# Attention loop's first iterations: bias vector by row sums, coupling ahead of the loop, value/output product over three iterations

## The reference, cut to what matters

```python
q = query @ Wq.T + bq                  # query = layernorm(x)
k = mem_state @ Wk.T + bk
v = mem_state @ Wv.T + bv
scores = einsum('btd,bsd->bts', q, k) / sqrt(d)   # only the 32 largest stay
attn = softmax(scores)
x = x + (attn @ v) @ Wo.T + bo
...
kernels = exp(-alpha * t) * cos(omega * t + phi)
kernels = kernels / clip(sum(abs(kernels)), 1e-8)
coupling = softmax(field_coupling)     # 16 x 16, mixes the heads of the wave
...
scale = max(mean(abs(W)), 1e-8)        # of each ternary weight
```

## Time and profile before

| what | value |
|---|---|
| three runs | 475.23, 476.73, 477.58 us (median 476.73) |
| the profiled execution | 476.81 us, of which its span is 474.9 |
| mean granted clock of TensorE | 0.996 |
| busy: PE, DVE, ACT, POOL | 450.1, 324.3, 253.7, 226.3 us |
| busy of PE's weight loads | 353.5 us |
| chain that ended last | PE 62%, DVE 20%, ACT 6%, issue 5%, POOL 4%, DMA 3% |

### The profile page before, as it was taken

One profiled execution on the slowest core, in us unless ns is written; L12 is line 12 of the kernel. 1 busy time (PEld: TensorE's weight loads), 2 busy tenths in 40 slices (PEclk: granted clock), 3 DMA queues, 4 the chain that ended last, 5 costly groups with the idle time before them and its releaser, 6 DMA issues.

```text
span 474.9 us, 6229 instructions
## 1 busy us (share of the span) xinstructions
PE 450.1 (95%) x2146; PEld 353.5 (74%) x2146; DVE 324.3 (68%) x582; ACT 253.7 (53%) x391; POOL 226.3 (48%) x265
## 2 busy tenths in 40 slices
PE   6999898899999899897899999999989999999996
PEld 2578565678888787685688888888768888888884
DVE  4899679698999899864898893655763322433223
ACT  1887857678888786673787546442551111211111
POOL 5703198379779767951000681334326653333330
PEclk9999999999999999899999999999999999999999
DMA  7997813153334324364372300000000000010002
GB/s 231 413 366 253 311 46 132 46 177 105 125 126 142 125 90 128 137 222 177 146 218 81 112 1 22 1 0 0 1 1 0 1 0 1 24 65 1 0 1 88
DMA packets 22814, 48.93 MB, mean 103 GB/s; under 512 B 2176, under 2 KB 2176, under 8 KB 21760
## 3 DMA queue, kind: packets, MB, share of 16 engines
q1 hardware_dynamic: 22784, 48.55, 29.1%
HBM read 46.44 MB, written 2.10 MB: 102 GB/s over the span
## 4 chain that ended last, share of the span: by engine, by line
PE 62%; DVE 20%; ACT 6%; issue 5%; POOL 4%; DMA 3%; DVEq 0%; SPq 0%; ACTq 0%; POOLq 0%
PE bank L1179 9%; PE bank L1181 9%; PE bank L1180 9%; PE bank L1584 6%; PE bank L1598 6%; PE bank L1600 6%; PE bank L1585 6%; DVE mt_lo L945 3%; PE bank L1194 3%; DMA ctxr<-ctx 3%; DVE work L958 2%; POOL nat_lo L418 2%; DVE mx L954 2%; PE bank L1186 2%; PE bank L1272 2%
## 5 line engine op out<-in xcount | busy, mean ns | idle before, releaser
L418 POOL TENSOR_TENSOR nat_lo<-ctxr,nat_hi 128x512 fp32r<-128x512 f32 x64 | 83.4, 1330 | 21.3 <-ACT nat_hi L600 20.9
L757 ACT ACTIVATE g<-bank,b1c 128x512 f32<-128x512 f32 x32 | 22.1, 691 | 91.2 <-PE bank L1600 91.2
L1159 DVE CAST g_hi<-g 128x512 fp32r<-128x512 f32 x32 | 13.7, 427 | 76.9 <-ACT g L757 76.8
L471 POOL TENSOR_SCALAR w2s<-w2t 128x512 fp32r<-128x512 int8 x32 | 19.9, 622 | 68.2 <-PE bank L1585 68.2
L1584 PE MATMUL bank<-w2s,g_lo 128*128 128x512 f32 x128 | 50.2, 392 | 1.8 <-DVE g_lo L1161 1.8
L1598 PE MATMUL bank<-xt_lo,w1s 128*128 128x512 f32 x128 | 50.8, 397 | 0.0
L1600 PE MATMUL bank<-xt_hi,w1s 128*128 128x512 f32 x128 | 50.7, 396 | 0.0
L1585 PE MATMUL bank<-w2s,g_hi 128*128 128x512 f32 x128 | 50.2, 392 | 0.0
L576 ACT ACTIVATE mt_hi<-bank 128x512 fp32r<-128x512 f32 x64 | 37.8, 596 | 20.2 <-PE bank L1350 19.7
L945 DVE TENSOR_TENSOR mt_lo<-bank,mt_hi 128x512 fp32r<-128x512 f32 x64 | 43.6, 682 | 5.9 <-ACT mt_hi L576 5.5
L1350 PEld LDWEIGHTS bank<-ident,ctxr 128*128 128x128 f32 x256 | 30.5, 141 | 15.4 <-DMA ctxr<-ctx 4.9
(11 more groups left out here) (233 smaller groups left out, 1204.0 us busy)
## 6 DMA issues: line engine op xcount, KB each, us to landing
ctxr<-ctx SPq DMA_DIRECT2D x32, 512.0 KB, 3.5
wab<-w1T SPq DMA_DIRECT2D x4, 1024.0 KB, 10.9
wab<-w2T SPq DMA_DIRECT2D x4, 1024.0 KB, 5.5
wgraw<-wgT SPq DMA_DIRECT2D x4, 1024.0 KB, 5.4
wst<-w1T SPq DMA_DIRECT2D x4, 1024.0 KB, 4.8
wst<-w2T SPq DMA_DIRECT2D x4, 1024.0 KB, 5.4
resid<-x SPq DMA_DIRECT2D x4, 512.0 KB, 6.5
out<-resid SPq DMA_DIRECT2D x8, 256.0 KB, 2.2
```

What stands on the lines that cost most here:

```text
L418: pool.tensor_tensor(nat_lo[:, par, c, :], ctxr[:, b % 4, c, :], f(nat_hi[:, par, c, :]), ALU.subtract).then_inc(nat_lo_ok, 1)
```

## The change

The bias vector's product is formed by row sums: DVE scales and adds the rows of `woraw` into `sum_k` (`xbias_sum`, four operations, ahead of the loop), and PE sums that over the partitions with one matmul against ones, now into bank 3 and after `score(0)`. The vector goes to a free tile `xn[:, 1]`, and POOL adds it to one tile of `resid` at the end of each iteration 1 to 8. The coupling's matmul goes ahead of `q_product(6)`, `mix_part` ahead of `kern`. In iteration 0 `norms` goes before `chunk(3)`. Of `wvo`, four matmuls go to iteration 0 (after `score` of steps 5 to 7), eight to iteration 1, four stay in iteration 2; quarter 1 goes to bank 4 and the quarters 0, 2 and 3 to bank 5, so quarter 3 waits for `wvo_lo_ok` 3. The sums of the ternary scales go to the head of iteration 1, and `turn_prob(0)` to its end.

```diff
+        def wvo_bank(d):
+            return bank[4 if d == 1 else 5]
...
POOL
-            def attn_bias(ts):
-                for t in ts:
+            def attn_bias(t):
+                if 0 <= t < NT:
                     pool.wait_ge(xbias_ok, 1)
                     pool.wait_ge(ln_ready, t + 1)
-                    pool.tensor_tensor(resid[:, t, :], resid[:, t, :], bias_x[:, :], ALU.add).then_inc(xres_ok, 1)
+                    pool.tensor_tensor(resid[:, t, :], resid[:, t, :], xn[:, 1, :], ALU.add).then_inc(xres_ok, 1)
...
                 split_q(i + 1, 0)
-                if i == 0:
-                    attn_bias(range(NT))
                 nat_lo_part(i - 1, 1)
+                attn_bias(i - 1)
...
ACT
                 mt_hi_part(0)
-                if i == 2:
-                    wvo_hi_part(2)
+                if i in (1, 2):
+                    wvo_hi_part(2 * i - 2)
...
                 nat_hi_part(i - 1, 1, (0, 1))
-                mt_hi_part(6)
                 if i == 1:
                     wvo_hi_part(1)
+                mt_hi_part(6)
...
DVE
+            def xbias_sum():
+                dve.wait_ge(wo_in, 16)
+                dve.wait_ge(qbias_ok, 1)
+                for o in range(DC):
+                    row_sum(sum_k, woraw, 2, o).then_inc(sums_ok, 1)
+                    dve.wait_ge(sums_ok, DC + o + 1)
...
             for t in range(4):
                 token_part(t)
+            mix_part()
... (kern, habs and its absolute value as before)
+            xbias_sum()
...
iteration 0 of DVE, before: m0 t4 m1 t5 m2 xbias m3 t6 t7 m4 mix m5 m6 norm ctok m7 sum_rows
iteration 0 of DVE, after:  m0 t4 m1 t5 m2 t6 m3 t7 ctok m4 xbias m5 norm m6 m7 sum_rows
(m = mt_lo_part, t = token_part; in iteration 1 wvo_lo_part(0) follows scales, wvo_lo_part(1) goes before m6)
-                    if p == 0:
-                        dve.wait_ge(xres_ok, NT)
+                    dve.wait_ge(xres_ok, p + 1)
...
PE
             for n in range(3, 2 * DC):
+                if n == 6:
+                    pe.wait_ge(cpr_ok, 2)
+                    pe.wait_ge(qbias_ok, 1)
+                    pe.matmul(bank[4][:, 0:H], cpr[0:H, :], ident[0:H, 0:H], start=True, stop=True).then_inc(coup_ps, 1)
                 q_product(n)
             def x_bias():
-                for o in range(DC):
-                    ins = pe.matmul(bank[4][:, :], cols[:, 2, o:o + 1].to_broadcast([P, P]), woraw[:, o, :], ...)
+                pe.wait_ge(sums_ok, 2 * DC)
+                pe.wait_ge(q_ok, 2 * DC)
+                pe.matmul(bank[3][:, :], ones[:, :].to_broadcast([P, P]), sum_k[:, :], start=True,
+                          stop=True).then_inc(xbias_ps, 1)
...
             def wvo_step(d, vs):
+                if d == 0 and vs[0] == 0:
+                    pe.wait_ge(wo_in, 16)
+                    pe.wait_ge(wv_in, 16)
+                    pe.wait_ge(ctok_sum, NT)
+                if d == 1 and vs[0] == 0:
+                    pe.wait_ge(mix_ok, 1)
+                    pe.wait_ge(norm_ok, 1)
+                    pe.wait_ge(scale_ok, 1)
+                if d >= 2 and vs[0] == 0:
+                    pe.wait_ge(wvo_lo_ok, 1 if d == 2 else 3)
...
             def wvo_in_turn(i, j):
+                if i == 0 and j >= 5:
+                    wvo_step(0, ((0,), (1,), (2, 3))[j - 5])
                 if i == 1:
                     if j == 0:
+                        totals()
+                    elif j < 4:
+                        wvo_step(1, ((0,), (1, 2), (3,))[j - 1])
                     else:
+                        wvo_step(2, (j - 4,))
                 if i == 2 and j < 2:
                     wvo_step(3, (2 * j, 2 * j + 1))
...
-                if i == 2:
-                    turn_prob(0)
...
                 join(i - 2, 1)
-                if i != 1:
-                    turn_prob(i - 1)
+                turn_prob(i - 1)
```

More of the change, by code:

```diff
@@ L512, in wvo_hi_part @@
                 act.wait_ge(wvo_ps, d + 1)
-                act.activation(wvo_hi[:, d, :], bank[4 + d % 2][:, :], ACT.Copy).then_inc(wvo_hi_ok, 1)
+                act.activation(wvo_hi[:, d, :], wvo_bank(d)[:, :], ACT.Copy).then_inc(wvo_hi_ok, 1)
             def first_tiles(ts):
@@ L895, in xbias_part @@
                 dve.wait_ge(bo_in, 16)
-                dve.tensor_tensor(bias_x[:, :], bias_x[:, :], bank[4][:, :], ALU.add).then_inc(xbias_ok, 1)
+                dve.wait_ge(ctok_sum, NT)
+                dve.tensor_tensor(xn[:, 1, :], bias_x[:, :], bank[3][:, :], ALU.add).then_inc(xbias_ok, 1)
             def mix_part():
@@ L915, in wvo_lo_part @@
                 dve.wait_ge(wvo_hi_ok, d + 1)
-                dve.tensor_tensor(wvo_lo[:, d, :], bank[4 + d % 2][:, :], f(wvo_hi[:, d, :]),
+                dve.tensor_tensor(wvo_lo[:, d, :], wvo_bank(d)[:, :], f(wvo_hi[:, d, :]),
                                   ALU.subtract).then_inc(wvo_lo_ok, 1)
@@ L997, in _ @@
                 if i == 0:
-                    token_part(6)
                     token_part(7)
-                if i == 1:
-                    wvo_lo_part(0)
+                    dve.wait_ge(ctok_sum, NT)
+                    dve.tensor_scalar(ctok[:, :], ctok[:, :], qbias[:, DC:DC + 1], None, ALU.add).then_inc(ctok_ok, 1)
+                    dve.wait_ge(ctok_ok, 1)
                 if i == 2:
@@ L1006, in _ @@
                 if i == 0:
-                    mix_part()
+                    xbias_part()
                 top8(i - 1, 2)
                 mt_lo_part(5)
-                top8(i - 1, 3)
-                mt_lo_part(6)
                 if i == 0:
                     norm_part()
-                    dve.wait_ge(ctok_sum, NT)
-                    dve.tensor_scalar(ctok[:, :], ctok[:, :], qbias[:, DC:DC + 1], None, ALU.add).then_inc(ctok_ok, 1)
-                    dve.wait_ge(ctok_ok, 1)
+                top8(i - 1, 3)
+                if i == 1:
+                    wvo_lo_part(1)
+                mt_lo_part(6)
                 p = i - 1
@@ L1265, in norms, with totals @@
                 pe.wait_ge(mix_ok, 1)
-                pe.matmul(bank[4][:, 0:P], ones[:, :].to_broadcast([P, P]), habs[:, :, :].rearrange("p h c -> p (h c)"),
-                          start=True, stop=True).then_inc(norm_ps, 1)
-            def wvo_step(d, vs):
+                pe.matmul(bank[4][:, P:2 * P], ones[:, :].to_broadcast([P, P]),
+                          habs[:, :, :].rearrange("p h c -> p (h c)"), start=True, stop=True).then_inc(norm_ps, 1)
+            def totals():
+                pe.wait_ge(abs_ok, 2 * DC)
+                pe.wait_ge(norm_ok, 1)
+                pe.matmul(bank[4][:, 2 * P:2 * P + 2 * DC], ones[:, :].to_broadcast([P, P]), wabs[:, :], start=True,
+                          stop=True).then_inc(abssum_ps, 1)
+            def wvo_step(d, vs):
+                if d == 0 and vs[0] == 0:
[4 more added lines that the diff above has]
+                    pe.wait_ge(mix_ok, 1)
+                    pe.wait_ge(norm_ok, 1)
+                    pe.wait_ge(scale_ok, 1)
+                if d >= 2 and vs[0] == 0:
+                    pe.wait_ge(wvo_lo_ok, 1 if d == 2 else 3)
                 for v in vs:
-                    ins = pe.matmul(bank[4 + d % 2][:, :], wvraw[:, v, token(d)], woraw[:, v, :], start=(v == 0),
+                    ins = pe.matmul(wvo_bank(d)[:, :], wvraw[:, v, token(d)], woraw[:, v, :], start=(v == 0),
                                     stop=(v == DC - 1))
@@ L1446, in _ @@
                 if i == 0:
-                    x_bias()
+                    norms()
                 chunk(3)
@@ L1451, in _ @@
                 weigh(i - 2, 0, 1)
+                if i == 0:
+                    x_bias()
                 chunk(4)
@@ L1458, in _ @@
                     project(i - 3, (2, 3))
-                if i == 0:
-                    coupling()
                 chunk(5)
```

70 lines of the change are left out of this document (17 added, 53 removed).

## The result

| | changed kernel | kernel before |
|---|---|---|
| median | 479.27 us (478.09 to 480.24, 6 executions) | 476.43 us (475.23 to 478.07, 6) |
| ratio | 1.0054, 95% interval 1.0037 to 1.0072 | |
| the profiled execution | 480.24 us, span 477.8 | 476.81 us, span 474.9 |
| mean granted clock of TensorE | 0.991 | 0.996 |
| busy: PE, DVE, ACT, POOL | 449.9, 324.2, 253.1, 226.1 us | 450.1, 324.3, 253.7, 226.3 us |

The account below looks back on a forecast made before the run. A ring of `weigh`, `nat_hi`, `nat_lo` and context load was taken to pace iterations 2 and 3, later DVE, POOL at the loop's end. 476.8 - 0.3 (front) + 0.1 (drift) + 1.2 (tail) = 477.8 us, range 473.4 to 480.2.

Parts of the forecast that it names:

- Tail: Loop's end: `attn_bias(7)` directly before the `rstd` at 201.34 delays everything behind; cost 1.2 us, between 0.4 and 1.25.
- Drift: From iteration 4 on, POOL's bias adds sit ahead of `split_q` and `rstd`; cost 0.1 us, between 0 and 0.5.
- Front: Ahead of the loop through iteration 2: reordered work starts chunk 0 of iteration 2 at 79.6, not 79.90; gain 0.3 us.
- the stall for `wvraw`: Iteration 0: PE reaches the first `wvo` matmuls at 55.5, before the load and eighth token sum; stall 1.0 us.
- quarter 1's: Iteration 1: quarter 1 waits for `scale_ok`, given after three small operations at 64.25; stall 0.55 us.
- the exponential's 3.57 us: Iteration 1: ACT's `nat_hi`, table load and exponential between the copies of chunks 3 and 4; 3.58 us in a row.
- The 10.65 us to the end of `weigh` (0,1): Iteration 2: both kernels need 10.65 us from chunk 0 to there, which releases the ring of `nat_hi`, `nat_lo`, load.
- rival B: Before `turn_prob(0)` and soon after: PE idling lowers the granted clock, 1.8 us on top, 479.6 us; chance 0.23.
- Rival A: Iteration 0: PE sheds its longest wait and three matmuls, 4.2 us, and the gain stays; 473.9 us; chance 0.20.
- C: Loop's end: another wait hides ACT's late `xn`, so the 1.2 us is gone; 476.6 us; chance 0.10.

Follow-up runs that it names:

- e9: Kernel before with the bias vector copied to `xn[:, 1]`, tiles 0 to 6 biased at iteration 0, tile 7 at the end of iteration 8; 481.44 us, ratio 1.0103.
- e11: Changed kernel, spread bias kept, plus the early one-column Exp and quarter 3 one chunk later; 476.39 us, ratio 1.0008.
- e1: Changed kernel, but POOL adds the bias to tile 7 at the end of iteration 1 instead of 8; 477.71 us, ratio 1.0026.
- e3: Changed kernel, but bias tiles 0 to 2 at the end of iteration 0 and 3 to 7 of iteration 1; 477.33 us, ratio 1.0023.
- e5: e3 with quarter 3 of the value/output product one chunk later in iteration 2; 476.80 us, ratio 1.0019.
- e10: Repeat of e3, the changed kernel with all bias tiles at the ends of iterations 0 and 1; 477.46 us, ratio 1.0028.
- e4: Changed kernel plus eight unused 128x512 matmuls on PE in the wait before `turn_prob(0)`; 478.89 us, ratio 1.0049.
- e6: e3 plus an Exp on one 128x1 column in iteration 1, so ACT loads its table while idle; 475.81 us, ratio 0.9988.
- e7: e3 with both the early one-column Exp and quarter 3 one chunk later; 475.31 us, ratio 0.9975.
- a2_after: The changed kernel itself measured again, nothing altered; 478.76 us, ratio 1.0045 against the kernel before.
- e8_table_before: Kernel before with only the early one-column Exp in iteration 1; 476.07 us, ratio 0.9987.
- e2: Kernel before with the vector copied to `xn[:, 1]` and one bias tile at the end of each of eight iterations, old front; 478.96 us, ratio 1.0051.

## Why the prediction was right in sign and short in size

**Tail: right.** Forecast 1.2; the distance is 18.23 to 18.30 us in all six profiles in which tile 7's bias stands there, against 17.04, and 17.03 to 17.04 in the seven others. `wk_lo` kept its 3.15 us, as the prediction had it: POOL's masks moved along.

**Drift: right.** Forecast 0.1, bound 0 to 0.5. From the `ln_rs` of iteration 4 to that of iteration 8 it is 67.36 us after and 67.11 before, but the second profile of the changed kernel has 67.11 too, so the 0.25 is no drift. It comes from one iteration that waited for a slow load of context:

```profile
158.77 0.66 PE L1354 MATMUL bank<-ident,ctxr 128*128 128x128 f32 x4 [1.73 <-DMA ctxr<-ctx]
```

That load took 5.30 us, where other loads on the chain took 3.4 to 3.6; in the kernel before one took 5.00 and PE waited 1.42 at 157.82. Twelve of the fourteen profiles have one or two such slow loads (4.4 to 5.4 us) on the chain in this part of the loop; those of e9 and e11 have none, and this part is 1.1 to 2.1 us shorter in them. The steps without a slow load, from one `ln_rs` to the next, are 16.55 to 16.68 us with the spread bias and 16.64 to 16.72 without; the last, to iteration 8, is 15.5 in all. POOL's idle time ahead of these rows went from 1.01 to 1.63 down to 0 to 0.41. It was the cover, as forecast, with little left.

**Front: the schedule right, the term wrong.** Up to 79.60 us each landmark came within 0.4 us of the forecast: the stall for `wvraw` (1.0 forecast, 1.06), quarter 1's (0.55, 0.43), the exponential's 3.57 us, `turn_prob(0)` at 78.99 for 79.1. The largest miss is PE's wait ahead of it, 2.00 for 2.5, since PE was through with its `wvo` matmuls at 76.99, not at 76.6. The 10.65 us to the end of `weigh` (0,1) were 10.73 at full clock. But the term "gain of the front: 0.3" was a cost of 0.9 to 1.1 in the median.

The step that failed is that I priced the 2.0 us of idling ahead of `turn_prob(0)` and the stall behind it at nothing in the forecast and put them into rival B with a chance of 0.23, as if the clock fell always or never. It falls in some executions. There are six profiles with the 2.0 us wait (two of the changed kernel, e1, e3, e5, e10). Four of them show the 0.50 behind it, at a cost of 0.63 to 0.65 us three times and of 2.52 once; e3 and e5 do not show it. The four profiles in which the wait was filled or cut to 0.95 us (e4, e6, e7, e11) do not show it either, nor do the four with the old order. B's 1.8 us lies between the two sizes.

I had priced nothing at all at the other new wait, 0.8 to 1.3 us for the load ahead of chunk 24: behind it the clock fell in a2_after and e4_fill, for some 1.5 us. Over the six profiles both falls together make 1.0 us on average, and the schedule without them gains 0.2 (79.60 and 10.73 make 90.33, and `weigh` ended at 90.55 before). This estimate, 0.8 us of loss from six single executions, is close to the 0.9 to 1.1 of the medians.

The series say the same less sharply. Of 66 executions of versions with the 2.0 us wait, 33 had a mean granted clock below 0.995; of 36 with the wait at 0.95 (e6, e7, e11), 7; of 12 of e8_table_before and 98 of the kernel before, none. But the mean does not say where the clock fell. e2 and e9 have no such wait and reach 5 of 12 and 3 of 6 (their profiles show a fall near 60 us), and e4, with the wait filled, 5 of 12. Nor does a low mean tell the cost. A fall near 200 us is in the profiles of the kernel before, the changed kernel, e2, e10 and e11 and in no other, and the tail is the same with it (17.04 and 18.23 to 18.26) as without it (17.03 to 17.04 and 18.27 to 18.30), since POOL, not PE, is what the chain waits for there. In the changed kernel the nine executions with the low mean and the nine others have medians of 478.8 and 478.7, and over all 66 the two halves differ by 0.95.

What stays open is how often each fall happens, which six profiles can't tell, and the 0.5 us and more behind the last matmul: the full-clock profile of e3_early ends its last matmul only 0.10 later than before (470.80 against 470.70), yet its span is 0.7 longer.

The new wait for `wvraw` costs little by itself but passes its scatter on. The first `wvo` matmul starts at 56.2 to 57.3 us in the ten profiles with the new front, ended by the load in some and by DVE's last token sum in others, whereas the load had 5 us of slack before; and chunk 0 of iteration 2 follows it by 22.9 to 23.1 us in each of the seven without the early table (21.9 to 22.1 in the three with it). In e3_early the load was issued at 49.0 instead of 48.2 and everything up to that chunk is 0.6 to 0.7 later than in the changed kernel.

**Rival A, the front's gain comes through: wrong for this change, right about where the gain was.** Its condition, that ACT's exponential did not delay chunk 4, was false, and e6_table shows what it is worth once made true: 1.6 us on the new front by the medians, of the 4.2 that it counted on. **C** fell with e1_tail.

## What to carry to other kernels

A serial add put in front of the last statistic of a loop costs its full length, and nothing in the iterations in which its engine idles: put such work where the engine has idle time, and look at the last iteration by itself. Reordering ahead of a bottleneck pays only when what bounds it is moved as well; here a 1.28 us table load, triggered in 2.3 us of idle time by an activation of one column, turned a loss of 1 us into none (475.81 against 476.50, an interval that holds no change), and with the quarter moved as well into a gain of 1.2. An idle stretch of TensorE for which nothing waits can still cost time behind it, where TensorE is what the chain waits for next, as behind 79.6 us; it costs nothing where another engine is, as near 200. Read the granted clock in the stretch behind it, in several profiles.

## What was not expected of the hardware

- Whether and for how long the granted clock falls behind a wait is a matter of the execution: the changed kernel has means of 0.991 to 1.000, and behind the same 2.0 us wait the profiles show no fall (e3), one of some 3 us (the changed kernel) and one of over 6 us (e1). Where the wait was 0.95 us, the share of executions with a low mean was one fifth instead of one half; that the wait alone makes this difference is not shown, since filling it by hand (e4_fill) left 5 of 12. The Trainium skill (TensorE: Matmul & The Clock Gate, What's actually happening) calls the phase at which the activity is looked at free-running; that executions of one kernel differ agrees with it.
- Beside POOL's adds of 1.25 us some DVE operations grew by up to 1 us, whatever their own length: a 128x128 subtraction took 0.29 us alone (e2_spread) and 1.25 us beside them, a 128x2 scalar operation (`winv`) 0.17 in the changed kernel and 1.18 in e9_tail_alone. For small operations in a chain that is a factor of 4 to 7. A copy of 0.43 us that pushed such a chain into that stretch, and the fall of the clock behind it, cost 2.3 us at chunk 16.
